# Gated cross-attention and mixture-of-experts block: another order within the attention slots, and the expert weights' low part subtracted on GpSimd

## What is computed

```python
def reference(x, ctx, g_xattn, g_ffn, Wq, bq, Wkv, bkv, Wout, bout, Wg, W1, b1, Wo, bo):
    # cross-attention, 16 heads of 8, keys and values from ctx
    q = layernorm(x) @ Wq + bq
    k, v = split(ctx @ Wkv + bkv)
    attn = softmax(einsum('bhid,bhjd->bhij', q, k) * 8 ** -0.5)
    x = x + tanh(g_xattn[0]) * (einsum('bhij,bhjd->bhid', attn, v) @ Wout + bout)
    # 8 experts, top 2 by the gate, their weights normalised to 1
    xn = layernorm(x)
    comb = top2(softmax(xn @ Wg.T))
    out = 0
    for e in range(8):
        a, b = split(xn @ W1[e].T + b1[e])          # 2 x 256 columns
        out += ((a * sigmoid(b)) @ Wo.T + bo) * comb[..., e:e+1]
    return x + tanh(g_ffn[0]) * out
```

## Time and profile before

| what | value |
|---|---|
| median of 3 runs | 126.2 us |
| the three runs | 124.78, 126.20, 126.21 us |
| the profiled execution, its own time | 124.31 us |
| its span | 122.2 us |
| TensorE clock granted, mean | 0.998 |
| busy: PE, PEld | 111.3, 76.7 us |
| busy: DVE, ACT, POOL | 99.6, 66.1, 83.7 us |

### The profile page before, as it was taken

How to read it: one execution, slowest core, us unless ns; L and a number is a source line. 1 busy time by engine, 2 the same in 40 slices (tenths; PEclk the granted TensorE clock), 3 DMA queues, 4 the chain that set the end, 5 groups by cost and what they waited for, 6 DMA issues and landing times.

```text
span 122.2 us, 2512 instructions
## 1 busy us (share of the span) xinstructions
PE 111.3 (91%) x808; PEld 76.7 (63%) x810; DVE 99.6 (81%) x274; ACT 66.1 (54%) x145; POOL 83.7 (68%) x106
## 2 busy tenths in 40 slices
PE   6989798899699979797979999999999799999982
PEld 2254554466466646564746877878686687878661
DVE  5489999779897989898795969599999778776770
ACT  3166467849586866675768266543433334343520
POOL 6359879997989599984235587857273987574600
PEclk9999999999999999999999999999999999999999
DMA  3999970000000000000000000000000000000001
GB/s 92 325 360 414 421 303 5 0 0 8 0 3 0 0 8 0 0 5 0 0 0 0 0 5 3 0 21 0 21 5 3 21 20 2 0 24 0 21 0 43
DMA packets 3468, 6.53 MB, mean 53 GB/s; under 512 B 384, under 2 KB 2048, under 8 KB 3456
## 3 DMA queue, kind: packets, MB, share of 16 engines
q1 hardware_dynamic: 3024, 5.66, 12.8%
q10 hardware_dynamic: 432, 0.72, 1.7%
HBM read 5.85 MB, written 0.52 MB: 52 GB/s over the span
## 4 chain that ended last, share of the span: by engine, by line
PE 52%; DVE 29%; issue 11%; ACT 4%; POOL 2%; DVEq 0%; ACTq 0%; POOLq 0%
PE ps L955 11%; PE ps L957 10%; PE ps L956 10%; DVE neg_max L613 9%; DVE gl L685 3%; PE ps L974 2%; PE ps L927 2%; DVE qk_lo L600 2%; PE ps L904 2%; DVE w_lo L796 2%; DVE max_m L792 2%; PE ps L1094 2%; ACT sig L448 1%; PE ps L984 1%; DVE att L783 1%
## 5 line engine op out<-in xcount | busy, mean ns | idle before, releaser
L328 POOL TENSOR_TENSOR gacc<-gacc,gl 128x256 f32<-128x256 f32 x38 | 28.6, 753 | 12.9 <-DVE gl L685 9.4
L448 ACT ACTIVATE sig<-ps 128x512 f32<-128x512 f32 (+1 forms) x33 | 19.3, 585 | 28.3 <-PE ps L957 25.8
L685 DVE SCALAR_TENSOR_TENSOR gl<-ps,comb,sig 128x256 f32<-128x256 f32 (+1 forms) x57 | 24.6, 471 | 5.0 <-ACT sig L448 4.7
L955 PE MATMUL ps<-w_hi,x_hi 128*128 128x512 f32 x64 | 27.3, 427 | 0.0
L956 PE MATMUL ps<-w_lo,x_hi 128*128 128x512 f32 x64 | 25.3, 395 | 0.0
L957 PE MATMUL ps<-w_hi,x_lo 128*128 128x512 f32 x64 | 25.3, 395 | 0.0
L394 ACT ACTIVATE probs<-ps 128x1024 f32<-128x1024 f32 x16 | 16.4, 1024 | 7.7 <-PE ps L914 7.5
L613 DVE TENSOR_REDUCE neg_max<-ps 128x8 f32<-128x1024 f32 x16 | 19.4, 1215 | 0.7 <-PE ps L887 0.6
L955 PEld LDWEIGHTS ps<-w_hi,x_hi 128*128 128x128 f32 x64 | 12.1, 188 | 3.0 <-DVE gl L685 0.6
L957 PEld LDWEIGHTS ps<-w_hi,x_lo 128*128 128x128 f32 x64 | 12.0, 188 | 2.9
L956 PEld LDWEIGHTS ps<-w_lo,x_hi 128*128 128x128 f32 x64 | 12.1, 190 | 1.9
(11 more groups left out here) (126 smaller groups left out, 209.4 us busy)
## 6 DMA issues: line engine op xcount, KB each, us to landing
w<-in_w1t SPq DMA_DIRECT2D x4, 512.0 KB, 9.0
w1l<-in_w1s SPq DMA_DIRECT2D x4, 512.0 KB, 9.5
out<-y SPq DMA_DIRECT2D x8, 64.0 KB, 1.5
cts<-in_ctx ACTq DMA_DIRECT2D x1, 384.0 KB, 5.6
pk<-in_pack SPq DMA_DIRECT2D x1, 332.0 KB, 5.7
xs<-in_x SPq DMA_DIRECT2D x2, 128.0 KB, 3.8
xs<-in_x SPq DMA_DIRECT2D x1, 256.0 KB, 5.3
wproj<-in_wqkv ACTq DMA_DIRECT2D x1, 192.0 KB, 3.2
```

The lines of the kernel that those rows point to most:

```text
L328: nc.gpsimd.tensor_tensor(gacc[:, t % 2, :], gacc[:, t % 2, :], gl[:, e - 1, :], ALU.add).then_inc(pool_experts_added, 1)
L448: nc.scalar.activation(sig[:, n % 3, e[0]:e[1], :], ps[:, b + e[0]:b + e[1], HH:H2], ACT.Sigmoid).then_inc(act_sigmoids, 1)
L685: nc.vector.scalar_tensor_tensor(dst[:, c[0]:c[1]], ps[:, 2 * (n % 3) + e % 2, c[0]:c[1]], comb[:, t, e:e + 1], sig[:, n % 3, e % 2, c[0]: ...
L955: mm(o, x_hi[:, t, :], w_hi[:, e, :], start=True, stop=False)
```

## The change

Three things are changed; what is computed stays.

First, w_lo moves from DVE (L796) to POOL: in step i, behind `keys_masked(i + 2)`, waiting for ACT's w_hi(i). PE's experts wait for the new semaphore.

Second, the order within a slot. On PE, `weighted(i - 1, 1)` comes right behind `scores(i, 0)`, ahead of the value projection and the output projection; the turn of the values (now `turn_values`) comes ahead of `scores(i, 1)` and the turn of att (`turn_attended`) right behind it, ahead of `weighted(i, 0)` and of the turn of the maxima. The turn of xn2 (`turn_xn2`) stays ahead of `scores(i, 0)` in even slots and comes behind it in odd ones. On DVE the reciprocal comes behind stats of tile i - 2, att behind its aggregate, and both ahead of the second maximum; in slot 7 they now stand ahead of the routing. In odd slots x_lo comes behind the first maximum. `low_parts` goes to the end of the even slots. On ACT `values_out` goes ahead of `values_in`.

Third, small moves at the start: bvl and var_eps of the last four tiles behind the second maximum of slot 0, the value bias (L1066, L769) from slot 0 to slot 1, and the zero matmuls of slot 1 go.

In this odd slot no turn of att or xn2 stands between the maxima and the next scores any more. The diff, cut to its core:

```diff
-        WARM = (4, 0)
+        WARM = 4
@@ POOL, in the loop
+                if on(i):
+                    pool.wait_ge(act_w1_high, i + 1)
+                    nc.gpsimd.tensor_tensor(w_lo[:, i, :], w1[:, i, :], w_hi[:, i, :].bitcast(fp32),
+                                            ALU.subtract).then_inc(pool_w1_low, 1)
@@ ACT, in the loop
+                if on(i - 1) and i < T:
+                    values_out(i - 1)
                 if i % 2 == 0 and on(i + 2):
                     values_in((i + 2) // 2)
-                if on(i - 1) and i < T:
-                    values_out(i - 1)
@@ DVE, new helpers
+            def inverse_sums(t):
+                dve.wait_ge(pe_values_turned, t + 1)
+                sums_inverted[0] = mark(nc.vector.reciprocal(rd, attended_heads()[:, :, :, HD]))
+            def attended(t):
+                if t >= 2:
+                    dve.wait_ge(pe_attended_turned, t - 1)
+                dve.wait_ge(dve_chain, sums_inverted[0])
...
@@ DVE, in the loop
+                    moments2 = mark(nc.vector.bn_stats(stats2[:, t % 2, :], x1[:, t, :]))
+                if on(i - 1) and i < T:
+                    inverse_sums(i - 1)
...
+                    moments2 = mark(nc.vector.bn_aggr(mv2[:, t % 2, :], stats2[:, t % 2, :]))
+                if on(i - 1) and i < T:
+                    attended(i - 1)
...
-                if on(i):
-                    dve.wait_ge(act_w1_high, i + 1)
-                    nc.vector.tensor_tensor(w_lo[:, i, :], w1[:, i, :], w_hi[:, i, :].bitcast(fp32),
-                                            ALU.subtract).then_inc(dve_w1_low, 1)
@@ PE, new helper
+            def turn_values(t):
+                pe.wait_ge(act_values, t + 1)
+                if t == 0:
+                    pe.wait_ge(dve_bout_scaled, 1)
+                else:
+                    pe.wait_ge(dve_x1, t)
...
@@ PE, in the loop
+                if on(i - 3) and (i % 2 == 0 or i >= T):
+                    turn_xn2(i - 3)
                 if on(i):
                     scores(i, 0)
...
+                if i % 2 == 1 and 3 <= i < T:
+                    turn_xn2(i - 3)
...
+                if on(i - 1) and i < T:
+                    weighted(i - 1, 1)
...
+                if on(i - 1) and i < T:
+                    turn_values(i - 1)
                 if on(i):
                     scores(i, 1)
+                if on(i - 1) and i < T:
+                    turn_attended(i - 1)
```

More of the change, by code:

```diff
@@ L575, in link, with mark, moments, variances @@
                 dve.wait_ge(dve_chain, chain[0])
-            def statistics(n):
+            def mark(ins):
+                chain[0] += 1
+                ins.then_inc(dve_chain, 1)
+                return chain[0]
+            def moments(n):
+                dve.wait_ge(x_loaded[n], 16)
+                for t in range(GROUPS[n], GROUPS[n + 1]):
+                    last = nc.vector.bn_stats(stats[:, t, :], xs[:, t, :])
+                return mark(last)
+            def variances(n, done):
                 tiles = range(GROUPS[n], GROUPS[n + 1])
-                dve.wait_ge(x_loaded[n], 16)
-                for t in tiles:
-                    last = nc.vector.bn_stats(stats[:, t, :], xs[:, t, :])
-                link(last)
+                dve.wait_ge(dve_chain, done)
                 for t in tiles:
@@ L842, in turn_xn, with turn_attended, turn_xn2 @@
                 last.then_inc(pe_xn_turned, 1)
+            def turn_values(t):
[4 more added lines that the diff above has]
+                    pe.wait_ge(dve_x1, t)
+                for k in range(2):
+                    last = nc.tensor.transpose(ps[:, VEB, P * k:P * (k + 1)],
+                                               o_sb[:, t % 2, P * k:P * (k + 1)], ident)
+                last.then_inc(pe_values_turned, 1)
+            def turn_attended(t):
+                pe.wait_ge(dve_attended, t + 1)
+                pe.wait_ge(act_v, min((t + 1) // 2 + 2, NP))
+                if t >= 2:
+                    pe.wait_ge(act_logits, t - 1)
+                nc.tensor.transpose(ps[:, AB, 0:P], att[:, t % 2, :], ident).then_inc(pe_attended_turned, 1)
+            def turn_xn2(t):
+                i = t + 3
+                if i <= T + 1:
+                    pe.wait_ge(act_attended, i - 1)
+                else:
+                    pe.wait_ge(act_gated, 1)
+                pe.wait_ge(act_normed2, t + 1)
+                nc.tensor.transpose(ps[:, AB, 0:P], xn2[:, t % 2, :], ident).then_inc(pe_xn2_turned, 1)
             def project(p):
@@ L1047, in _ @@
                        stop=True).then_inc(pe_attention_out, 1)
-                if on(i - 1) and i < T:
-                    weighted(i - 1, 1)
+                if i == 1:
+                    pe.wait_ge(act_out_weights, 1)
+                    pe.wait_ge(dve_v_bias, 1)
+                    pe.wait_ge(dve_max_masked, 2)
+                    mm(ps[:, VEB, 0:D], bvl[:, :], wout_t[:, :], start=True, stop=True).then_inc(pe_value_bias, 1)
                 if i == T - 1:
@@ L1059, in _ @@
                     logits(i - 3)
+                if on(i - 1) and i < T:
+                    turn_values(i - 1)
                 if on(i):
                     scores(i, 1)
-                if i == 0:
-                    pe.wait_ge(act_out_weights, 1)
-                    pe.wait_ge(dve_v_bias, 1)
-                    pe.wait_ge(dve_max_masked, 1)
-                    mm(ps[:, VEB, 0:D], bvl[:, :], wout_t[:, :], start=True, stop=True).then_inc(pe_value_bias, 1)
-                if on(i - 1):
-                    t = i - 1
-                    pe.wait_ge(act_values, t + 1)
-                    if t == 0:
-                        pe.wait_ge(dve_max_masked, 2)
-                    else:
-                        pe.wait_ge(dve_x1, t)
-                    for k in range(2):
-                        last = nc.tensor.transpose(ps[:, VEB, P * k:P * (k + 1)],
-                                                   o_sb[:, t % 2, P * k:P * (k + 1)], ident)
-                    last.then_inc(pe_values_turned, 1)
+                if on(i - 1) and i < T:
+                    turn_attended(i - 1)
+                if i == T:
+                    turn_values(T - 1)
                 if on(i):
                     weighted(i, 0)
-                if on(i):
-                    pe.wait_ge(act_v, min(i // 2 + 2, NP))
-                    if i >= 3:
-                        pe.wait_ge(act_logits, i - 2)
-                    keep_busy(WARM[0] if i < 2 else WARM[1], AB)
+                if i == 0:
+                    pe.wait_ge(act_v, 2)
+                    keep_busy(WARM, AB)
                 if i == T:
```

112 lines of the change are left out of this document (52 added, 60 removed).

## The result

The changed kernel takes 133.45 us (median of four runs: 132.16, 132.54, 134.36, 142.71), the kernel before, on the same chip at the same time, 125.49 (124.03 to 126.21). The ratio is 1.064 (95% interval 1.049 to 1.079). The forecast was 129.0, with a range up to 132: the direction held, the size was short by 4.4. The four runs had a mean granted clock of 0.961, 0.948, 0.933 and 0.843; the ratio compares the two fastest runs of each kernel (132.16 and 132.54 with 124.03 and 124.78).

The account below looks back on a forecast made before the run. The prediction took DVE's chain to set the 5.90 us slot, with POOL nearly full and becoming the bound after the change. +3.7 up to slot 7 and -0.2 behind it gave +3.5 on 125.5, so 129.0 us, range 125.5 to 132.

Parts of the forecast that it names:

- (a): On DVE, w_lo's eight instructions leave: worth at most 0.84 a slot, nothing where PE or ACT wait for POOL.
- (b): On POOL, w_lo arrives as eight new instructions, taken at 1.26 us each start to start.
- (c): On POOL, q_lo_m shortens from 1.45 to 1.00 start to start once w_lo no longer runs on DVE.
- the step: POOL's work per slot becomes 6.38 us against a slot of 5.90, so POOL becomes the bound within two slots.
- The rival that w_lo would cost 1.00: POOL binds but w_lo costs 1.00 instead of 1.26: +1.9, 127.4 us; chance 22%.
- (d): At the start, POOL idles 1.5 us, from 18.4 to 19.85, ahead of w_lo(0), waiting for ACT's w_hi(0).
- the sum: POOL's durations and the new waits added up along the slots: +3.7 up to slot 7, -0.2 behind it, +3.5 together.
- (e): POOL's durations summed from 19.85: w1(6) ends at 57.72, slot 7 starts no earlier than 59.74, +2.6.
- (f): New waits for var2 on DVE: only slot 4 leaves POOL idle, 1.0; slot 7 starts at 60.8, +3.7.
- (g): Slot 7 and behind: PE's wait for att goes, -0.2; later routing costed at nothing.
- the third: Slower still: q_lo_m stays at 1.45 (+1.8) or later routing is on the path (+1.1): +5.5, 131.0 us; chance 14%.
- the second: Faster: PE's order decides, five slots gain about 0.4 each and the start 0.7: -2.7, 122.8 us; chance 9%.

Follow-up runs that it names:

- e8: Kernel before, in its old order, with w_lo taken off DVE and put late on POOL, in steps 7 and 8: 129.95 us, ratio 1.040.
- e11: Kernel before without its four idle matmuls of slot 1: 124.97 us, ratio 1.000.
- e4: Changed kernel with no w_lo computed; the expert product that read it reads w_hi instead: 126.64 us.
- e6: As e4, with six idle matmuls added in slot 1: 124.15 us, ratio 0.992.
- e14: Changed kernel with only six idle matmuls added, all in slot 1: 138.08 us in the median.
- e2: Kernel before with only w_lo moved from DVE to POOL, old order kept: 134.66 us, ratio 1.082.
- e7: Changed kernel with slot 1 filled by idle matmuls and all w_lo late on POOL, around w1(7) and behind slot 7: 127.71 us, ratio 1.027.
- e13: Changed kernel with idle matmuls in slots 1 and 2 and three to one behind the maxima in slots 1 to 6: median 130.49 us, ratio 1.039.
- e9: Changed kernel with idle matmuls in slots 1 and 2 and eight behind the turn of the maxima in slots 1 to 6: 132.77 us.

## Why the prediction came out as it did

- (a) w_lo leaves DVE: held, nearly nothing. In the old order (e8) it is 0.5 over seven slots.
- (b), (c) and the step: held. 1.27 against 1.26; q_lo_m at 1.03 or 1.04 in all eight; step 6.33 against 6.38. The rival that w_lo would cost 1.00 falls by this row.
- (d) POOL idle ahead of w_lo(0): 1.50 as forecast, but it ended at 20.83 instead of 19.85. Of this 1.0, 0.6 is a later start of this execution (slot 0 at 12.51; the kernel before had 11.90), which no step of the sum could know; the rest is not explained.
- (e) held until slot 3: w1(1), w1(2) and w1(3) start at 24.06, 31.84 and 38.20, and the forecast's sum has 23.1, 30.9 and 37.3, each 0.9 to 1.0 earlier, the delay of (d). From there the sum fails: w1(4) starts at 46.38, 8.2 behind w1(3), where POOL's step is 6.33.
- (f) the waits for var2: forecast as one of 1.0 in slot 4. Measured 1.81 in slot 3 and 2.59 in slot 4 (ahead of rstd at 50.25), both because PE was late: in slot 3 by the low clock, and slot 4 began 4.0 behind the forecast while POOL's w1(4), at 46.38, was only 2.7 behind its 43.7. Slot 4 was to start near 41.8 and started at 45.81; slot 7 near 60.8 and started at 64.89. The miss is 4.0 at slot 4 and 4.1 at slot 7, so all of it lies ahead of slot 4. By the forecast's own terms slot 3 starts at 34.2 (w1(2) ends at 32.2, scores follow 2.0 later) and is 7.6 long; it started at 34.73. So 0.5 is there before slot 3, and the other 3.5 arise in it, at a clock of 0.54.
- (g) behind slot 7 the forecast was -0.2, and it was +0.4. WARM's four matmuls were costed at nothing. In the old order that is right (e11). In the new one a filled slot 1 was worth 126.64 - 124.15 = 2.5 us when nothing else made PE wait (e4, e6), and nothing that can be seen when POOL did (e14).

The step that failed is the sum itself, as (e) and (f) draw it: "+3.7 - 0.2 = +3.5". It took every PE duration from rows at a granted clock of 1.00, and then let PE wait for POOL in slots 2 and 3 (1.18 and 1.69 measured), without a term for what the wait does to the matmuls behind it. POOL as the bound was right (e2, e7, e13's chain) and its price nearly so: 4.1 with the clock held (e13, one run), 3.5 forecast. The missing term is the clock. In the medians it is 133.45 - 125.49 - 4.1 = 3.9; in the profiled execution it is the 3.5 of slot 3, of which the rows of e13 and e9 give 3.2 to the clock. Within the four runs of the changed kernel the time goes with the time at half clock: 10, 14, 18 and 44 us of it, and 132.2, 132.5, 134.4 and 142.7 us. A straight line through the first and the last, (142.71 - 132.16) / (44.2 - 10.2) = 0.31 us for each, leads back to 129.0 without any. That this is the number forecast is luck to some degree, but it agrees with e13's 128.4. The slope is this kernel's alone: in e13, with its idle matmuls in the chain, 3.3 us at half clock went with 1.8 us more (130.24 against 128.44).

Of the rivals, the third named the size nearest to the truth (131.0) for reasons that did not occur: q_lo_m went to 1.04, and what is behind slot 7 cost 0.4 and not 1.1. Its 1.8 for q_lo_m was also counted short: the sum takes the short time in step 6 as well, where the kernel before has a long one (1.49 at 51.24), so four steps should be five, 2.2. Nothing spoke for the second.

What stays open: why an episode at half clock lasts 10 us in one run and 31 in another of the same kernel, and why the same waits in the kernel before (0.82 at 31.57) mostly pass without a fall. e13's term of 4.1 rests on one run, and the price of slot 3 on one profiled execution of each kernel.

## What to carry to other kernels

An operation moved to an engine that is "68% busy" must be added to that engine's step in the stage where it lands, and the step compared with the slot; here 5.57 + 1.26 - 0.45 against 5.90 told the direction and the size of the engine's own term. Then, where the new bound makes TensorE wait in several slots running (here 0.5 to 1.7 us, five times in three slots), look at the granted clock behind the waits, and price them twice: once by their length, and once by the matmuls behind them at half speed. Idle matmuls must stand where the waits are: in slot 1 alone they held the clock when that was the place where it fell (e6) and did nothing when waits followed (e14); filling about half of each wait held it in one run of four (e13), and eight a slot held it and took the bound themselves (e9).
